# Full-width operations in the projection stage of an attention and FFN kernel, and a column sum taken from float32 tiles

## The chip, the cores and the metric

The kernel runs on all 8 NeuronCores of one Trainium2 chip. Each core takes 2 of the 16 sequences and does the whole computation on them; the cores exchange nothing. The metric is the device time in microseconds (us) of the slowest core.

## The reference

The input x is 16 sequences of 2048 tokens with 1024 features, in float32. The first half is an attention over the 16 heads of each single token, not over the tokens, and a layer norm:

```python
Q = (x @ Wq.T).reshape(b, s, h, hd)      # h = 16, hd = 64; K and V likewise
scores = jnp.einsum('bshd,bstd->bsht', Q, K) / math.sqrt(hd)
attn = jax.nn.softmax(scores, axis=-1)
out = jnp.einsum('bsht,bstd->bshd', attn, V).reshape(b, s, dm)
x = _layernorm(x + out @ Wfc.T)
```

The second half takes the mean of that x over the tokens of a sequence and puts it through a small net, which gives one number `gf` per sequence. Then three cycles follow, in which a four-layer net gives one number per token, and every token is updated with it:

```python
global_context = x.mean(axis=1, keepdims=True)
gf = _global_net(global_context, ...)
for _ in range(3):
    tf = _coupling_net(out, ...)
    coupling = 0.1 + adaptive_range * (0.7 * gf + 0.3 * tf - 0.5) * 2.0
    out = out + coupling * _twist(out)
x = _layernorm(x + out)
```

## The kernel before

Every engine has its own list of small functions, and the order in which Python appends to these lists is the order of the engine's queue. Waits are written out by hand, as semaphores with counts. Work is done one sequence (a batch of 2048 tokens) after the other, in three stages.

The **attention stage** takes the tokens in four blocks of 512. TensorE makes Q, K and V (L458); VectorE multiplies Q by shifted copies of K (L518, L524), and TensorE sums the products over the 64 features of a head with an indicator matrix (L544), which leaves the scores in `pS`, two PSUM banks of 512 columns. Then comes a chain in which each step waits for the one before: ScalarE takes the exponential of both banks into `praw` (`acE`, L565 and L566), TensorE sums it (L578, L579), ScalarE makes the reciprocals (L586 to L592), TensorE spreads them over the partitions with two float32 matmuls (L600, L601), VectorE multiplies (`dvN`, L610 and L611). After that TensorE spreads the weights (L643, 32 rows of the array), ScalarE copies them out (L659), VectorE multiplies them with V (L674), and TensorE sums again (L690, 64 columns of the array). The chain runs 8 times in all, 4 times for each batch.

The **projection stage** takes the tokens in 16 tiles of 128 (variable `tt`). For one tile TensorE does two groups of 8 full matmuls (`pe3`, L799), one for each half of the 1024 output columns, into two of the four banks of `pBIG`. VectorE adds the residual `x0f32` to each half (`dv2`, L811) into `sumtile`, takes mean and variance (`dv3`, L823 to L826), and ScalarE makes the reciprocal deviation (`ac3`, L834, L838). VectorE then writes the normalized tile twice (`dv4`): in float32 into `x1` (L849), which stays in SBUF for the rest of the batch, and in bfloat16 into `x1bfgc` (L852), a buffer for one tile. Two matmuls (`pe4`, L758 and L760) with a column of ones as stationary operand add the columns of `x1bfgc` into the sum over the tokens, of which the mean is made later. One tile's two matmuls accumulate on those of the tile before, in `pR` and `pA`.

The functions `dv4` and `pe4` of a tile are appended one tile late: VectorE's queue has `dv2` and `dv3` of tile tt, then `dv4` of tile tt-1; TensorE's queue has `pe3` of tile tt, then `pe4` of tile tt-1, then `pe3` of tile tt+1. For the last tile `dv4` also waits for the `pe4` before it (the count `gcg`). The sync engine's queue loads `x0f32` for tile tt when the additions of tile tt-1 are done.

The **FFN stage** transposes the tiles by DMA, runs the small net on the sum, and then runs the three cycles. It has its own epilogue with a layer norm, and is not touched by the change.

Of the kernel before, what the change touches and what calls it, by code (L numbers as in the profile page):

```python
# [7 lines left out]
F32 = mybir.dt.float32  # L8
BF16 = mybir.dt.bfloat16
AF = mybir.ActivationFunctionType  # L10
ALU = mybir.AluOpType
# [5 lines left out]
EXP_SCALE = 0.125  # L17
# [21 lines left out]
def build_nc():  # L39
# [31 lines left out]
    def at(name, shape, dtype, align=64):  # L71
        o = (off[0] + align - 1) // align * align
        t = nc.alloc_sbuf_tensor_at(name, shape, dtype, offset=BASE + o)
        nbytes = 1
        for s_ in shape[1:]:
            nbytes *= s_
        nbytes *= mybir.dt.size(dtype)
        off[0] = o + nbytes
        return t
# [4 lines left out]
    onesb = at("onesb", [128, 128], BF16)  # L84
# [4 lines left out]
    lncol = at("lncol", [128, 4], F32)  # L89
# [11 lines left out]
    expb = at("expb", [128, 1], F32)  # L101
# [9 lines left out]
    gw3sb = at("gw3sb", [128, 2], BF16)  # L111
    lnb = at("lnb", [8, 512], F32)
    idf32 = at("idf32", [128, 128], F32)
    tanhrow = at("tanhrow", [1, 256], F32)
    c4row = at("c4row", [1, 256], F32)
    assert off[0] <= 18000, off[0]
# [81 lines left out]
    pS = pBIG  # L198
# [70 lines left out]
    def ve_init(v):  # L269
        v.wait_ge(s_const.h, 1)  # L270
        v.memset(onesb[:, :], 1.0)
        v.memset(onesf[:, :], 1.0)
        v.memset(expb[:, :], EXP_BIAS)
        v.memset(epscol[:, :], LN_EPS)
        v.tensor_scalar(rcol[:, 1:2], rcol[:, 0:1], 64.0, None, ALU.is_ge)
        v.drain()
        for t in range(16):
            v.tensor_scalar(iwork2[:, 0:1], rcol[:, 1:2], 16.0, float(t), ALU.mult, ALU.add)
            v.drain()
            v.tensor_scalar(iwork2[:, 32:64], iwork[:, 0:32], iwork2[:, 0:1], None, ALU.is_equal)  # L280
            v.drain()
            v.tensor_copy(indt[:, t * 32: t * 32 + 32], iwork2[:, 32:64])
            v.drain()
        v.tensor_scalar(iwork2[:, 0:1], rcol[:, 1:2], -64.0, rcol[:, 0:1], ALU.mult, ALU.add)
        v.drain()
        v.tensor_scalar(iwork2[:, 1:65], iwork[:, 0:64], iwork2[:, 0:1], None, ALU.is_equal)
        v.drain()
        v.tensor_copy(redd[:, :], iwork2[:, 1:65])
        v.drain()
        v.tensor_scalar(iwork2[:, 0:1], rcol[:, 0:1], 1.0 / 16.0, None, ALU.mult)  # L290
        v.drain()
        v.tensor_scalar(iwork2[:, 8:16], iwork[:, 0:8], -1.0, iwork2[:, 0:1], ALU.mult, ALU.add)
        v.drain()
        v.tensor_scalar(iwork2[:, 16:24], iwork2[:, 8:16], 0.0, None, ALU.is_ge)
        v.tensor_scalar(iwork2[:, 24:32], iwork2[:, 8:16], 1.0, None, ALU.is_lt)
        v.drain()
        v.tensor_tensor(iwork2[:, 32:40], iwork2[:, 16:24], iwork2[:, 24:32], ALU.mult)
        v.drain()
        v.tensor_copy(rind[:, :], iwork2[:, 32:40])
        v.drain()  # L300
        v.tensor_scalar(iwork2[:, 0:128], iwork[:, 0:128], 1.0 / 16.0, None, ALU.mult)
        v.drain()
        v.tensor_scalar(iwork2[0:8, 0:128], iwork2[0:8, 0:128], rcol[0:8, 0:1], None, ALU.subtract)
        v.drain()
        v.tensor_scalar(iwork[0:8, 0:128], iwork2[0:8, 0:128], 0.0, None, ALU.is_ge)
        v.tensor_scalar(iwork2[0:8, 0:128], iwork2[0:8, 0:128], 1.0, None, ALU.is_lt)
        v.drain()
        v.tensor_tensor(e8[:, :], iwork[0:8, 0:128], iwork2[0:8, 0:128], ALU.mult)
        v.drain()
        nc.vector.engine_nop().then_inc(s_const.h, 1)  # L310
# [57 lines left out]
    for b in range(B_LOC):  # L368
# [26 lines left out]
        for sb_ in range(NSB):  # L395
# [165 lines left out]
            def acE(a, sacc_final=sacc_final, png=pnorm_gate_prev):  # L561
                a.wait_ge(s_sacc.h, sacc_final)
                if png > 0:
                    a.wait_ge(s_pnorm.h, png)
                a.activation(praw[:, 0:512], pS[:, 0:512], AF.Exp, bias=expb[:, :], scale=EXP_SCALE)  # L565
                a.activation(praw[:, 512:1024], pS[:, 512:1024], AF.Exp,  # L566
                             bias=expb[:, :], scale=EXP_SCALE).then_inc(s_exp2.h, 1)
            P.act.append(acE)
            exp_t = s_exp2.inc()
# [36 lines left out]
            def dvN(v, rexp_t=rexp_t, pfm_reuse=pfm_reuse):  # L606
                v.wait_ge(s_rexp.h, rexp_t)
                if pfm_reuse > 0:
                    v.wait_ge(s_pexp.h, pfm_reuse)
                v.tensor_tensor(pfm[:, 0:512], pBIG[:, 1024:1536], praw[:, 0:512], ALU.mult)  # L610
                v.tensor_tensor(pfm[:, 512:1024], pBIG[:, 1536:2048], praw[:, 512:1024],  # L611
                                ALU.mult).then_inc(s_pnorm.h, 1)
            P.dve.append(dvN)
            pnorm_t = s_pnorm.inc()
# [128 lines left out]
        def emit_dv4(gcg=0, P=P):  # L743
            fn, tt_p = pend_dv4[0]
            if gcg > 0:
                def wrapped(v, fn=fn, gcg=gcg):
                    v.wait_ge(s_gcs.h, gcg)
                    fn(v)
                P.dve.append(wrapped)
            else:  # L750
                P.dve.append(fn)
            x1_t = s_x1.inc()

            def pe4(te, x1_t=x1_t, tt=tt_p, rcp_gate=s_rcp2.n):
                te.wait_ge(s_x1.h, x1_t)
                if tt == 0:
                    te.wait_ge(s_rcp2.h, rcp_gate)
                m1 = te.matmul(pR[0:1, 0:512], onesb[:, 0:1], x1bfgc[:, 0:512],  # L758
                               start=(tt == 0), stop=(tt == NTT - 1))
                m2 = te.matmul(pA[0:1, 0:512], onesb[:, 0:1], x1bfgc[:, 512:1024],  # L760
                               start=(tt == 0), stop=(tt == NTT - 1))
                m2.then_inc(s_gcs.h, 1)
            P.pe.append(pe4)
            s_gcs.inc()
            pend_dv4[0] = None
            return x1_t

        for tt in range(NTT):
# [17 lines left out]
            for half in range(2):  # L786
                slot = slot0 + half
                bfree = fc_bank_free[slot]

                def pe3(te, tt=tt, half=half, slot=slot, ao_done=ao_done, bfree=bfree,  # L790
                        first=(tt == 0 and half == 0), wfc_tgt=wfc_tgt):
                    if first:
                        te.wait_ge(s_aoev.h, ao_done)
                        te.wait_ge(s_wf2.h, wfc_tgt)
                        te.wait_ge(s_winit.h, N_WINIT)
                    if bfree > 0:
                        te.wait_ge(s_sum.h, bfree)
                    for c in range(8):
                        mm = te.matmul(SLOT[slot],  # L799
                                       attnoutT[:, c * 2048 + tt * 128: c * 2048 + tt * 128 + 128],  # L800
                                       wfcsb[:, c * 1024 + half * 512: c * 1024 + half * 512 + 512],
                                       start=(c == 0), stop=(c == 7))
                    mm.then_inc(s_fc.h, 1)
                P.pe.append(pe3)
                fc_t = s_fc.inc()

                def dv2(v, fc_t=fc_t, x0f_t=x0f_t, half=half, tt=tt, slot=slot,
                        fsem=fsem, stile=stile):
                    v.wait_ge(s_fc.h, fc_t)
                    v.wait_ge(fsem.h, x0f_t)  # L810
                    v.tensor_tensor(stile[:, half * 512: half * 512 + 512],  # L811
                                    SLOT[slot],
                                    x0f32[:, (tt % 2) * 1024 + half * 512: (tt % 2) * 1024 + half * 512 + 512],
                                    ALU.add).then_inc(s_sum.h, 1)
                P.dve.append(dv2)
                sum_t = s_sum.inc()
                fc_bank_free[slot] = sum_t
            x0f_gate_prev = sum_t

            def dv3(v, sum_t=sum_t, par=par, stile=stile):  # L820
# [25 lines left out]
            def dv4(v, rstd_t=rstd_t, tt=tt, par=par, stile=stile):  # L846
                v.wait_ge(s_rstd.h, rstd_t)
                ag = aggr if par == 0 else aggr2
                v.tensor_scalar(x1[:, tt * 1024: tt * 1024 + 1024], stile[:, :],  # L849
                                ag[:, 0:1], lncol[:, par * 2 + 1: par * 2 + 2],  # L850
                                ALU.subtract, ALU.mult)
                v.tensor_scalar(x1bfgc[:, :], stile[:, :],  # L852
                                ag[:, 0:1], lncol[:, par * 2 + 1: par * 2 + 2],
                                ALU.subtract, ALU.mult)
                v.drain()
                nc.vector.engine_nop().then_inc(s_x1.h, 1)
# [658 lines left out]
```

## Time and profile before

| | |
|---|---|
| time, median of 3 runs | 3631.97 us (3628.18 to 3632.47) |
| the profiled execution's own time | 3658.85 us |
| its span on the slowest core | 3657.3 us (the fastest core: 3617.5 us) |
| granted TensorE clock, mean of the cores | 0.68 to 0.70 of full speed |
| PE, DVE, ACT busy | 66%, 37%, 32% of the span |
| projection stage, first batch | about 1008 to 1169 us |
| projection stage, second batch | about 2810 to 2978 us |

The profile is of one execution and one core (core 2). The clock column of the profile gives TensorE's granted clock as a share of 2.4 GHz: 1.00 is 2.4 GHz and 0.50 is 1.2 GHz. In the timeline a row is an instruction, or several of one kind merged, with its start and its length; what stands in brackets is how long the engine sat idle before it, and what ended that. Ends of matmuls are modelled, so for a chain of matmuls the distance between two starts says more than the lengths do.

### The profile page before, as it was taken

Reading aid. Unit: us, or ns where it says so; the run is one execution under the profiler, and the core shown is the slowest. Engines: PE = TensorE matmul, PEld = TensorE weight load, DVE = VectorE, ACT = ScalarE, POOL = GpSimd, SP = SyncE. Lnnn points to the kernel's source line nnn. Section 1 sums busy time; section 2 is a strip of 40 time slices with the busy share of each in tenths; the row PEclk is TensorE's granted clock in tenths of the full one; section 3 lists DMA queues with packets and bytes.
Section 4 is the critical chain, followed back from the end, with each engine's and each line's share of the span. In section 5 each row is a group of like instructions: output and inputs, shape, how many; then the busy total and the mean of one; then the engine's idle time right before and its main releaser. Section 6 shows DMA issues by size and latency. Waiting matters only on the chain.

```text
span 3657.3 us, 35637 instructions; the slowest of 8 cores (3617.5 to 3657.3 us)
## 1 busy us (share of the span) xinstructions
PE 2431.9 (66%) x10693; PEld 1064.8 (29%) x10736; DVE 1365.3 (37%) x2096; ACT 1163.9 (32%) x1848; POOL 37.6 (1%) x65
## 2 busy tenths in 40 slices
PE   0478788796754567575707887878876527585756
PEld 0221213122111345454503121221311105454544
DVE  2063544426343233333314425354343422423234
ACT  0125162442500233333301543516243003333333
POOL 1000000000000000000000000000000000000000
PEclk9955757575587777687757575565655867686877
DMA  6310100000112000100061001000001120101000
GB/s 90 57 33 1 21 1 1 1 1 12 21 49 53 9 18 18 35 5 31 3 109 35 18 3 19 1 1 1 12 1 29 52 46 4 35 3 33 8 28 24
DMA packets 110788, 83.88 MB, mean 23 GB/s; under 512 B 84496, under 2 KB 89104, under 8 KB 110608
## 3 DMA queue, kind: packets, MB, share of 16 engines
q0 software_dynamic: 19472, 31.21, 5.7%
q1 hardware_dynamic: 91136, 50.40, 4.8%
q8 instruction: 97, 1.59, 0.2%
q14 instruction: 83, 0.68, 0.1%
HBM read 79.18 MB, written 16.78 MB: 26 GB/s over the span
## 4 chain that ended last, share of the span: by engine, by line
PE 28%; DVE 5%; SPq 4%; DVEq 4%; issue 3%; ACT 3%; DMA 3%; ACTq 0%; POOLq 0%
PE pBIG L1151 5%; PE pQK L458 5%; PE pBIG L643 4%; SPq L934 3%; DVEq L514 2%; PE pBIG L799 2%; PE pQK L643 2%; PE pA L690 2%; PE pR L690 2%; PE pQK L1187 2%; SPq L424 1%; ACT pexpsb L659 1%; DMA outTbf<-xstg 1%; DMA x0tok<-x 1%; PE pBIG L544 1%
## 5 line engine op out<-in xcount | busy, mean ns | idle before, releaser
L674 DVE TENSOR_TENSOR prdsb<-pexpsb,vtsb 128x1024 bf16<-128x1024 bf16 x512 | 354.6, 693 | 534.3 <-ACT pexpsb L659 222.9
L1151 PE MATMUL pBIG<-outTbf,cw1sb 128*128 128x256 bf16 x3072 | 467.9, 327 | 41.4 <-ACT h1T L1164 41.3
L659 ACT ACTIVATE pexpsb<-pBIG 128x1024 bf16<-128x1024 f32 x344 | 349.2, 1023 | 159.3 <-PE pBIG L643 156.9
L1151 PEld LDWEIGHTS pBIG<-outTbf,cw1sb 128*128 128x128 bf16 x3072 | 344.7, 117 | 176.1 <-issue 69.6
L643 PE MATMUL pBIG<-pfm,expf 32*128 32x512 bf16 x688 | 345.4, 614 | 74.2 <-ACT pexpsb L659 60.8
L544 PE MATMUL pBIG<-prodb,indt 128*32 128x512 bf16 x1024 | 231.7, 550 | 144.9 <-DVE prodb L518 121.7
L458 PE MATMUL pQK<-x0T,wqsb 128*128 128x512 bf16 x497 | 129.5, 426 | 236.6 <-DMA x0T<-x0tok 233.8
L1164 ACT ACTIVATE h1T<-pBIG,cb1sb 128x256 bf16<-128x256 f32 x384 | 181.2, 473 | 261.9 <-PE pBIG L1151 261.8
L1187 PE MATMUL pQK<-h1T,cw2sb 128*128 128x256 bf16 x1536 | 182.4, 278 | 42.2 <-ACT h1T L1164 42.0
L510 DVE COPY kr<-ktsb 64x512 bf16<-64x512 bf16 x128 | 36.4, 285 | 440.5 <-ACT ktsb L471 438.6
L518 DVE TENSOR_TENSOR prodb<-qtsb,kr 128x2048 bf16<-128x2048 bf16 x128 | 156.8, 1225 | 101.5 <-PE pBIG L544 84.8
L643 PE MATMUL pQK<-pfm,expf 32*128 32x512 bf16 x336 | 172.6, 615 | 28.9 <-ACT pexpsb L659 28.9
L659 ACT ACTIVATE pexpsb<-pQK 128x1024 bf16<-128x1024 f32 x168 | 171.8, 1023 | 56.9 <-PE pQK L643 54.8
L1266 DVE TENSOR_SCALAR c4row<-tanhrow,abrow 1x256 f32<-1x256 f32 x48 | 19.2, 400 | 434.9 <-ACT tanhrow L1259 432.8
L544 PEld LDWEIGHTS pBIG<-prodb,indt 128*32 128x32 bf16 x1024 | 96.9, 100 | 279.2 <-issue 259.5
L690 PE MATMUL pR<-prdsb,redd 128*64 128x512 bf16 x512 | 162.7, 633 | 21.5 <-DVE prdsb L674 21.5
L799 PE MATMUL pBIG<-wfcsb,attnoutT 128*128 128x512 bf16 x500 | 152.0, 469 | 34.8 <-DMA wfcsb<-wfcT 33.4
L1187 PEld LDWEIGHTS pQK<-h1T,cw2sb 128*128 128x128 bf16 x1536 | 144.4, 99 | 80.2 <-issue 55.2
L690 PE MATMUL pA<-prdsb,redd 128*64 128x512 bf16 x512 | 162.8, 632 | 4.6 <-DVE prdsb L674 4.4
L1301 DVE TENSOR_TENSOR Ptw<-outT,C4N 128x512 f32<-128x512 f32 x192 | 119.8, 685 | 118.5 <-ACT C4N L1289 118.5
L524 DVE TENSOR_TENSOR prodb<-qtsb,kr 128x2048 bf16<-128x2048 bf16 x128 | 155.8, 1218 | 0.0
L458 PEld LDWEIGHTS pQK<-x0T,wqsb 128*128 128x128 bf16 x512 | 54.3, 108 | 311.1 <-issue 271.8
(176 smaller groups left out, 2024.7 us busy)
## 6 DMA issues: line engine op xcount, KB each, us to landing
x0f<-x SPq DMA_DIRECT2D x32, 512.0 KB, 3.2
out<-x2slab SPq DMA_DIRECT2D x32, 512.0 KB, 2.6
x0tok<-x POOLq DMA_DIRECT2D x32, 256.0 KB, 3.6
x0T<-x0tok SPq DMA_TRANSPOSE x256, 2.3
wqsb<-wqT POOLq DMA_DIRECT2D x2, 2048.0 KB, 18.6
wksb<-wkT POOLq DMA_DIRECT2D x2, 2048.0 KB, 30.5
wvsb<-wvT POOLq DMA_DIRECT2D x2, 2048.0 KB, 41.9
wfcsb<-wfcT POOLq DMA_DIRECT2D x2, 2048.0 KB, 16.3
```

Source lines behind the costliest of these rows:

```text
L458: mm = te.matmul(bank, wsb[:, (k * 8 + dch) * 128: (k * 8 + dch) * 128 + 128], x0T[:, par * 4096 + k * 512: par * 4096 + k * 512 + 512], s ...
L518: v.tensor_tensor(bass.AP(prodb, 0, [[4096, 128], [512, 4], [1, 512]]), bass.AP(qtsb, 0, [[4096, 128], [512, 4], [1, 512]]), krep, ALU.mul ...
L524: v.tensor_tensor(bass.AP(prodb, 2048, [[4096, 128], [512, 4], [1, 512]]), bass.AP(qtsb, 2048, [[4096, 128], [512, 4], [1, 512]]), krep, A ...
L544: mm = te.matmul(pS[32 * (c % 4): 32 * (c % 4) + 32, (c // 4) * 512: (c // 4) * 512 + 512], indt[:, t * 32: t * 32 + 32], prodb[:, c * 512 ...
L643: mm = te.matmul(pvb[:, hh * 512: hh * 512 + 512], expf[rb: rb + 32, (hh * 8 + k) * 128: (hh * 8 + k) * 128 + 128], pfm[rb: rb + 32, grp * ...
L659: a.activation(pexpsb[:, slot * 1024: slot * 1024 + 1024], pvb, AF.Copy).then_inc(s_pev.h, 1)
L674: v.tensor_tensor(bass.AP(prdsb, slot * 1024, [[2048, 128], [512, 2], [1, 512]]), bass.AP(pexpsb, slot * 1024, [[2048, 128], [512, 2], [1, ...
L690: te.matmul(rbank[hh * 64: hh * 64 + 64, :], redd[:, :], prdsb[:, slot * 1024 + hh * 512: slot * 1024 + hh * 512 + 512], start=(k == 0), s ...
L799: mm = te.matmul(SLOT[slot], attnoutT[:, c * 2048 + tt * 128: c * 2048 + tt * 128 + 128], wfcsb[:, c * 1024 + half * 512: c * 1024 + half ...
L1151: mm = te.matmul(SLOT[bank][:, 0:256], cw1sb[:, (k * 8 + dch) * 128: (k * 8 + dch) * 128 + 128], outTbf[:, k * 512 + hf * 256: k * 512 + h ...
L1164: a.activation(h1T[:, dch * 512 + hf * 256: dch * 512 + hf * 256 + 256], SLOT[bank][:, 0:256], AF.Gelu, bias=cb1sb[:, dch:dch + 1]).then_i ...
L1187: mm = te.matmul(pQK[:, q * 512: q * 512 + 256], cw2sb[:, (k * 4 + dch) * 128: (k * 4 + dch) * 128 + 128], h1T[:, k * 512 + hf * 256: k * ...
```

## The change

Four things are edited, and nothing else moves.

1. The exponential of the scores is one ScalarE instruction over 1024 columns, not two over 512.
2. The multiplication by the reciprocals (`dvN`) is one VectorE instruction over 1024 columns, not two.
3. The residual addition (`dv2`) of the projection stage is one instruction over 1024 columns. It is emitted after the second half's matmuls and waits for them, so the count on `s_sum` goes up once for each tile and not twice; both banks come free with it.
4. The bfloat16 copy `x1bfgc` is no longer written. `pe4` reads the float32 tile in `x1`, with a new float32 column of ones (`onec`, set once at the start) as stationary operand.

```diff
+    onec = at("onec", [128, 1], F32)
...
+        v.memset(onec[:, :], 1.0)
...
-                a.activation(praw[:, 0:512], pS[:, 0:512], AF.Exp, bias=expb[:, :], scale=EXP_SCALE)
-                a.activation(praw[:, 512:1024], pS[:, 512:1024], AF.Exp,
+                a.activation(praw[:, 0:1024], pS[:, 0:1024], AF.Exp,
                              bias=expb[:, :], scale=EXP_SCALE).then_inc(s_exp2.h, 1)
...
-                v.tensor_tensor(pfm[:, 0:512], pBIG[:, 1024:1536], praw[:, 0:512], ALU.mult)
-                v.tensor_tensor(pfm[:, 512:1024], pBIG[:, 1536:2048], praw[:, 512:1024],
+                v.tensor_tensor(pfm[:, 0:1024], pBIG[:, 1024:2048], praw[:, 0:1024],
                                 ALU.mult).then_inc(s_pnorm.h, 1)
...
-                m1 = te.matmul(pR[0:1, 0:512], onesb[:, 0:1], x1bfgc[:, 0:512],
+                m1 = te.matmul(pR[0:1, 0:512], onec[:, 0:1],
+                               x1[:, tt * 1024: tt * 1024 + 512],
                                start=(tt == 0), stop=(tt == NTT - 1))
-                m2 = te.matmul(pA[0:1, 0:512], onesb[:, 0:1], x1bfgc[:, 512:1024],
+                m2 = te.matmul(pA[0:1, 0:512], onec[:, 0:1],
+                               x1[:, tt * 1024 + 512: tt * 1024 + 1024],
                                start=(tt == 0), stop=(tt == NTT - 1))
...
+                if half == 1:
+                    def dv2(v, fc_t=fc_t, x0f_t=x0f_t, tt=tt, slot0=slot0,
+                            fsem=fsem, stile=stile):
+                        v.wait_ge(s_fc.h, fc_t)
+                        v.wait_ge(fsem.h, x0f_t)
+                        v.tensor_tensor(stile[:, :],
+                                        pBIG[:, slot0 * 512: slot0 * 512 + 1024],
+                                        x0f32[:, (tt % 2) * 1024: (tt % 2) * 1024 + 1024],
+                                        ALU.add).then_inc(s_sum.h, 1)
+                    P.dve.append(dv2)
+                    sum_t = s_sum.inc()
+                    fc_bank_free[slot0] = sum_t
+                    fc_bank_free[slot0 + 1] = sum_t
...
-                v.tensor_scalar(x1bfgc[:, :], stile[:, :],
-                                ag[:, 0:1], lncol[:, par * 2 + 1: par * 2 + 2],
-                                ALU.subtract, ALU.mult)
```

On VectorE, one tile in the middle of the projection stage (x1 stands as `x_113`, x0f32 as `x0f`) was this:

```order
L811 TENSOR_TENSOR sumtile<-pBIG,x0f_96 128x512 x2
L823 BN_STATS stats<-sumtile 128x6
L824 BN_STATS stats<-sumtile 128x6
L826 BN_AGGR aggr<-stats 128x2
L828 ISA
L849 TENSOR_SCALAR x_113<-sumtile_87,aggr_47,lncol 128x1024
L852 TENSOR_SCALAR x1bfgc<-sumtile_87,aggr_47,lncol 128x1024
L856 ISA
```

and is now this, with x1 as `x_114`:

```order
L814 TENSOR_TENSOR sumtile<-pBIG,x0f_97 128x1024
L827 BN_STATS stats<-sumtile 128x6
L828 BN_STATS stats<-sumtile 128x6
L830 BN_AGGR aggr<-stats 128x2
L832 ISA
L853 TENSOR_SCALAR x_114<-sumtile_88,aggr_47,lncol 128x1024
L857 ISA
```

The two additions have become one of twice the width, and one of the two full-width writes is gone. The order is otherwise the same.

On TensorE the same stage, from its first matmuls, was this:

```order
L799 MATMUL pBIG<-wfcsb,attnoutT 128x512 x32
L758 MATMUL pR<-x1bfgc,onesb 1x512
L760 MATMUL pA<-x1bfgc,onesb 1x512
L799 MATMUL pBIG<-wfcsb,attnoutT 128x512 x16
L758 MATMUL pR<-x1bfgc,onesb 1x512
L760 MATMUL pA<-x1bfgc,onesb 1x512
```

and is now this:

```order
L801 MATMUL pBIG<-wfcsb,attnoutT 128x512 x32
L758 MATMUL pR<-x_114,onec 1x512
L761 MATMUL pA<-x_114,onec 1x512
L801 MATMUL pBIG<-wfcsb,attnoutT 128x512 x16
L758 MATMUL pR<-x_114,onec 1x512
L761 MATMUL pA<-x_114,onec 1x512
```

No matmul has moved; the two of `pe4` read float32 operands of the same shapes.

## Rows read from the trace of the kernel before

**Rows 1.** The page: engines, and the clock over 40 slices.
```profile
PE 2431.9 (66%) x10693; PEld 1064.8 (29%) x10736; DVE 1365.3 (37%) x2096; ACT 1163.9 (32%) x1848; POOL 37.6 (1%) x65
PEclk9955757575587777687757575565655867686877
```
**Rows 2.** Timeline, one settled tile of the projection stage.
```profile
1042.12 0.58 PE L758 MATMUL pR<-x1bfgc,onesb 128*1 128x512 bf16 x1 [4.55 <-DVEq L856]
1042.49 0.63 PE L760 MATMUL pA<-x1bfgc,onesb 128*1 128x512 bf16 x1
1043.06 4.70 PE L799 MATMUL pBIG<-wfcsb,attnoutT 128*128 128x512 bf16 x16
...
1046.21 0.69 DVE L811 TENSOR_TENSOR sumtile<-pBIG,x0f 128x512 f32<-128x512 f32 x1 [4.34 <-PE pBIG L799]
1047.93 0.69 DVE L811 TENSOR_TENSOR sumtile<-pBIG,x0f 128x512 f32<-128x512 f32 x1 [1.03 <-PE pBIG L799]
...
1050.53 0.81 DVE L849 TENSOR_SCALAR x<-sumtile,aggr,lncol 128x1024 f32<-128x1024 f32 x1 [0.18 <-issue]
...
1051.26 0.81 DVE L852 TENSOR_SCALAR x1bfgc<-sumtile,aggr,lncol 128x1024 bf16<-128x1024 f32 x1
...
1052.31 0.59 PE L758 MATMUL pR<-x1bfgc,onesb 128*1 128x512 bf16 x1 [4.55 <-DVEq L856]
```
**Rows 3.** Stretches: start and end, length, then busy time of each engine, clock, DMA.
```profile
1035.10:1041.80 6.70, 2.47 (x12) 0.91 (x10) 4.34 (x7) 0.50 (x2) 0.00 (x0) 1.00 0.23 78
1041.90:1045.20 3.30, 3.08 (x8) 0.88 (x9) 0.00 (x0) 0.00 (x0) 0.00 (x0) 0.50 0.00 0
1045.30:1052.00 6.70, 2.46 (x12) 0.89 (x10) 4.35 (x7) 0.50 (x2) 0.00 (x0) 1.00 0.25 78
2827.10:2833.80 6.70, 5.67 (x14) 1.81 (x15) 1.37 (x2) 0.00 (x0) 0.00 (x0) 0.50 0.00 0
240.00:250.00 10.00, 9.59 (x26) 1.54 (x24) 4.84 (x7) 8.01 (x9) 0.53 (x1) 0.50 0.24 43
```
**Rows 4.** Timeline, first and last column sums of each batch.
```profile
1021.28 0.52 PE L758 MATMUL pR<-x1bfgc,onesb 128*1 128x512 bf16 x1 [4.66 <-DVEq L856]
1154.67 0.59 PE L758 MATMUL pR<-x1bfgc,onesb 128*1 128x512 bf16 x1 [4.55 <-DVEq L856]
1164.90 0.59 PE L758 MATMUL pR<-x1bfgc,onesb 128*1 128x512 bf16 x1 [4.55 <-DVEq L856]
1166.10 0.81 DVE L849 TENSOR_SCALAR x<-sumtile,aggr,lncol 128x1024 f32<-128x1024 f32 x1 [1.43 <-PE pA L760]
2828.13 0.59 PE L758 MATMUL pR<-x1bfgc,onesb 128*1 128x512 bf16 x1 [4.66 <-DVEq L856]
2829.07 5.97 PE L799 MATMUL pBIG<-wfcsb,attnoutT 128*128 128x512 bf16 x16
2974.05 0.58 PE L758 MATMUL pR<-x1bfgc,onesb 128*1 128x512 bf16 x1 [4.54 <-DVEq L856]
```
**Rows 5.** Groups by line: a float32 addition over 1024 columns.
```profile
L1388 DVE TENSOR_TENSOR sumtile<-x,sumtile 128x1024 f32<-128x1024 f32 x32 | 39.2, 1225 | 5.6 <-ACT sumtile L1378 3.1 <-issue 2.4
```
**Rows 6.** Timeline, the chain from the scores to the weights, first block.
```profile
228.23 0.69 ACT L565 ACTIVATE praw<-pBIG,expb 128x512 bf16<-128x512 f32 x1 [46.60 <-PE pBIG L544]
228.81 0.68 ACT L566 ACTIVATE praw<-pBIG,expb 128x512 bf16<-128x512 f32 x1
...
233.54 2.04 PE L600 MATMUL pBIG<-rcpf,e 8*128 8x512 f32 x2 [2.88 <-ACT rcpf L592]
...
235.37 1.91 PE L601 MATMUL pBIG<-rcpf,e 8*128 8x512 f32 x2
...
237.39 0.69 DVE L610 TENSOR_TENSOR pfm<-pBIG,praw 128x512 bf16<-128x512 f32 x1 [10.66 <-PE pBIG L601]
238.00 0.68 DVE L611 TENSOR_TENSOR pfm<-pBIG,praw 128x512 bf16<-128x512 f32 x1
```
**Rows 7.** Groups by line: ScalarE copies from PSUM of 1024 and of 512 columns.
```profile
L659 ACT ACTIVATE pexpsb<-pBIG 128x1024 bf16<-128x1024 f32 x344 | 349.2, 1023 | 159.3 <-PE pBIG L643 156.9 <-DVE prdsb L674 0.6
L471 ACT ACTIVATE ktsb<-pQK 128x512 bf16<-128x512 f32 x64 | 38.2, 597 | 77.6 <-PE pQK L458 77.6
```
**Rows 8.** Timeline, TensorE after the last column sum of batch 1.
```profile
1212.17 0.35 PE L984 MATMUL pQK<-onesb,gcrow 1*128 1x1 bf16 x8 [43.28 <-DVEq L978]
```
**Rows 9.** Timeline, the load of the residual for the next tile.
```profile
1038.51 10.52 SPq L779 DMA_DIRECT2D x0f<-x  x2
```

More of the change, by code:

```diff
@@ L805, in build_nc @@
                 fc_t = s_fc.inc()
[L807 to L817, printed above, removed]
+                if half == 1:
[11 more added lines that the diff above has]
+                    fc_bank_free[slot0 + 1] = sum_t
             x0f_gate_prev = sum_t
```

## The prediction

> **What bounds the kernel now.** I read the page first. TensorE is the busiest engine with 66% of the span, VectorE and ScalarE have 37% and 32%, and the clock row swings between 5 and 9 tenths [rows 1]. No engine is full, so a stage is set by chains of waits, and by which level of the clock TensorE has there. Each edit has to be read in its own stage.
>
> Next I read the timeline of one settled tile of the projection stage [rows 2]. It is a ring of serial work. TensorE starts `pe4` at 1042.12 and the 16 full matmuls (L799) at 1043.06, whose last ends just before VectorE's second addition at 1047.93. VectorE then adds, takes statistics and writes the previous tile twice, and only the end of the second write (L852) releases the next `pe4`, at 1052.31. In front of it TensorE has sat idle for 4.55 us. The ring takes 10.19 us: 0.94 for `pe4`, about 4.7 for the full matmuls, 4.55 for VectorE with TensorE idle. So every 0.1 us that VectorE loses behind the last full matmul, or TensorE gains in `pe4`, is paid 0.1 us a tile, unless the clock moves too.
>
> The clock does move. Between 1035.10 and 1041.80 it was 1.00 (2.4 GHz), between 1041.90 and 1045.20 it was 0.50 (1.2 GHz), then 1.00 again to 1052.00 [rows 3]. It falls near the end of TensorE's idle time, `pe4` and the first five or so full matmuls run at 1.2 GHz, and it comes back 2.2 us after the first full matmul. In the first tile of batch 2 the low stretch lasted from 2827.10 to 2833.80, because `pe4` began 1.1 us after the fall [rows 3, 4]: the clock came back only 4.8 us after the first full matmul (2829.07), and the 16 of them took 5.97 us instead of 4.70 [rows 4]. So the later in a low stretch the full matmuls start, the longer it lasts, and that is worth more than a microsecond.
>
> What raises the clock is not TensorE being busy as such. From 240 to 250 us it is busy for 9.59 us of 10 and the clock stays at 0.50 [rows 3]; the work there uses 32 rows (L643) or 64 columns (L690) of the array. `pe4` uses one column. I take it that `pe4` does nothing for the clock, in bfloat16 or in float32.
>
> **The change part by part.** *The additions.* Before, half of the addition was done while the second half's matmuls ran; 0.69 us stood behind them [rows 2]. Now all of it does. The same kind of operation over 1024 columns takes 1.225 us [rows 5]. So +0.53 us a tile in the ring. Behind the waiting addition on VectorE stand the statistics and `dv4`, all in the ring already. The bank of the first half comes free later, but it is needed only two tiles on. SP's load of the next residual is issued at the end of the addition, so 0.53 us later; it was issued at 1038.51 for additions from 1046 on [rows 2, 9], and stays hidden.
>
> *The second write.* L849 starts at 1050.53 and L852 at 1051.26 [rows 2]; without L852 the release comes that much earlier: −0.73 us a tile. TensorE's idle time becomes 4.55 + 0.53 − 0.73 = 4.35 us.
>
> *The column sums.* The trace shows no float32 matmul with one column. The nearest rows are L600 and L601, float32 over 512 columns at a clock of 1.2 GHz: each runs as two records, and the first starts 1.83 us before the second [rows 6]. A float32 matmul there costs over four times what a bfloat16 one does (0.38 from L758 to L760 [rows 2]). Their weights are 128 columns wide and here they are one, so I take 1.75 us each, 3.5 us for the pair, against 0.94 now: +2.55 us a tile at 1.2 GHz. The bounds are 0.94 us (float32 costs nothing here) and 3.7 us; at 2.4 GHz the pair would be near 1.8 us.
>
> *The full matmuls behind them.* Here the larger half of the uncertainty lies. With the fall where it is now or earlier, 3.5 us of one-column work at 1.2 GHz stand ahead of the full matmuls, so these begin later in the low stretch than in any tile of the trace, and the tile nearest to it is the first of batch 2, with 4.8 us of low clock behind the first full matmul and 5.97 us for the sixteen. The ends are 3.4 us (sixteen at 2.4 GHz: 16 × 0.215, from the spacing of the second half, 1.72 us between the two additions of a tile) and 6.8 us (all at 1.2 GHz). I take 5.8, a little under the row. That is +1.1 us a tile.
>
> The ring becomes 4.35 + 3.5 + 5.8 = 13.65 us. Its ends: 4.35 + 1.8 + 3.4 = 9.6 and 4.35 + 3.7 + 6.8 = 14.9.
>
> *Over the stage.* From the first `pe4` to the fifteenth are 14 rings in each batch: 1164.90 − 1021.28 = 143.6 us and 2974.05 − 2828.13 = 145.9 us now [rows 4]. With the first ring or two of each batch shorter before it settles, I take 189.5 us for each: +45.9 and +43.6, together +89.5 us. At the end `dv4` of the last tile waits for the fifteenth `pe4`: it started 1.20 us behind it [rows 4], now some 3.7, less the second write: +2.5 − 0.7 = +1.8 for each batch, +3.6. The last `pe4` itself is off the path: TensorE then waits 43.28 us for transposes by DMA and VectorE [rows 8]. The first tile's addition costs +0.4 for each batch, +0.8, before the ring begins.
>
> *The attention stage.* The exponentials take from 228.23 to 229.49, 1.26 us [rows 6]. A copy of 1024 columns takes 1.023 us, and the exponential needs 0.09 more than a copy (0.69 against 0.597) [rows 6, 7]: 1.11 us, −0.15. The multiplications take from 237.39 to 238.68, 1.29 us, against 1.225 [rows 5]: −0.07. Both stand on a chain that nothing covers, since the engines around them wait. Eight times −0.22 is −1.8 us. They can't lose more than they were.
>
> Sum: 89.5 + 3.6 + 0.8 − 1.8 = +92 us. On the profiled execution's 3658.85 us that is 3751; it was 27 us slower than the median, and 3631.97 + 92 = **3724 us**.
>
> **The rivals.** *A: float32 column sums raise the clock.* If 3.5 us of unbroken one-column work counted as activity, the clock would come back before the full matmuls: 4.35 + 3.5 + 3.4 = 11.3 us a ring, +1.1 × 28 = +31, and with the small terms +33: 3665 us. Rows 240 to 250 speak against it: nearly full, and at 0.50. The Trainium skill speaks for it: "TensorE: Matmul & The Clock Gate", Part 1, says that the activity monitor gates the clock on how busy the engine has been, and that sustained matmuls release it. By that rule alone the ring would be 11.3 us; the trace doesn't bear it out where the array is partly used. A mixed case, in which the rise alternates between early and late, lies around 12 us a ring, +50: 3684.
>
> *B: the clock never falls.* TensorE's idle time shrinks to 4.35 us. The last full matmul of the tile ended before 1047.93, and the clock was still 1.00 until 1052.00, over 4.1 us later [rows 2, 3], so the margin is small. If 4.35 us of idle time were too short for a fall, all would run at 2.4 GHz and the ring be 9.6 us, −0.6 × 28 = −17; the ends of the stages give nothing, the attention stage −1.8: −19 us, 3613, faster than before. It decides from the point where no fall shows in the idle time. Against it: what the clock has to be kept up by is the full matmuls, and between these now lie 4.35 + 1.8 = 6.2 us instead of 5.5.
>
> *C: float32 with one column costs as bfloat16.* Then the ring is 0.2 us shorter at most, −6 − 2: 3624; or, since the fall seems to hold the ring where it is (it crept up to 10.23 us, from 1154.67 to 1164.90 [rows 4]), −2: 3630. L600 and L601 speak against it.
>
> **How the numbers follow.** The forecast has a chance of 0.78, A with the mixed case 0.14, B 0.04, C 0.04. The forecast's own range is +78 (the clock returns a little earlier) to +108 us (settled from the first ring, on every core): 3710 to 3740. To leave out no more than 2 in 10 I go down to the mixed case, 3680, and up to 3748. What a measurement can tell from no change is 0.2%, 7 us. Faster by more: B and half of C, 0.05. Within: the rest of C, 0.03. Slower: 0.92.
>
> **What would show it.** Right: L758 and the second column sum appear as four records a tile, 3.4 to 3.6 us from the first to the first full matmul at a clock of 0.50; a ring of 13 to 13.7 us; TensorE's idle before L758 at 4.35; sixteen full matmuls at 5.5 to 6; two additions gone for one of 1.23 us; 46 us more between first and fifteenth `pe4` of a batch; all else unchanged. Wrong: `pe4` near 1 us (C), a clock of 1.00 at the first full matmul (A), or a clock of 1.00 all through a tile (B). The forecast would also fail if the stage's clock settled into another pattern, for which the trace of before gives no row.

## The result, and the profile after

The changed kernel takes 3699.69 us (median of 9 runs, 3681.84 to 3727.03), the kernel before 3632.22 us in the same sessions. The ratio is 1.0166, with a 95% interval from 1.0141 to 1.0191: about 60 us slower. In some executions one die of the chip has a lower clock and the time is 1 to 3% longer; the ratios leave these out, the medians don't. The forecast was slower by 92 us, 3724 us, in a range from 3680 to 3748. The direction and the place were right, and one step of the sum, the full matmuls behind the column sums, was too large.

The profile after is of core 7, with a span of 3692.3 us. These rows of its page answer to [rows 1]:

```profile
PE 2478.6 (67%) x10800; PEld 1054.6 (29%) x10800; DVE 1336.6 (36%) x2025; ACT 1163.8 (32%) x1840; POOL 37.5 (1%) x65
```

TensorE is busy 47 us longer and VectorE 29 us shorter; the two pages are of different cores, so this is rough. Next the timeline after: two tiles of the projection stage, matmuls and VectorE's addition. They answer to [rows 2].

```profile
1059.44 1.87 PE L758 MATMUL pR<-x,onec 128*1 128x512 f32 x2 [4.36 <-DVEq L857]
1061.10 1.91 PE L761 MATMUL pA<-x,onec 128*1 128x512 f32 x2
1062.94 4.45 PE L801 MATMUL pBIG<-wfcsb,attnoutT 128*128 128x512 bf16 x16
...
1067.58 1.22 DVE L814 TENSOR_TENSOR sumtile<-pBIG,x0f 128x1024 f32<-128x1024 f32 x1 [8.38 <-PE pBIG L801]
...
1070.70 0.81 DVE L853 TENSOR_SCALAR x<-sumtile,aggr,lncol 128x1024 f32<-128x1024 f32 x1 [0.18 <-issue]
...
1071.75 1.86 PE L758 MATMUL pR<-x,onec 128*1 128x512 f32 x2 [4.36 <-DVEq L857]
1073.41 1.76 PE L761 MATMUL pA<-x,onec 128*1 128x512 f32 x2
1075.11 3.63 PE L801 MATMUL pBIG<-wfcsb,attnoutT 128*128 128x512 bf16 x16
```

The float32 column sums appear as four records a tile and last from 1059.44 to 1062.94, 3.50 us, and from 1071.75 to 1075.11, 3.36 us. TensorE's idle time in front is 4.36 us. Both were forecast to within 0.15 us. The 16 full matmuls, though, take 4.45 and 3.63 us, in turn, and not 5.8. The stretches of the clock in the same two tiles answer to [rows 3] (length, busy time of PE, PEld, DVE, ACT, POOL, clock, DMA):

```profile
1057.90:1064.60 6.70, 5.16 (x8) 0.95 (x9) 1.05 (x3) 0.50 (x2) 0.00 (x0) 0.50 0.18 65
1064.70:1071.40 6.70, 2.70 (x13) 1.02 (x11) 3.42 (x5) 0.50 (x2) 0.00 (x0) 1.00 0.24 72
1071.50:1074.80 3.30, 3.05 (x4) 0.36 (x4) 0.01 (x1) 0.00 (x0) 0.00 (x0) 0.50 0.02 6
1074.90:1081.70 6.80, 3.84 (x17) 1.49 (x16) 2.56 (x4) 0.00 (x0) 0.00 (x0) 1.00 0.09 17
```

In the first tile the clock is at 1.2 GHz until 1.7 us behind the first full matmul (1062.94). In the second it is back at 2.4 GHz before the first full matmul at 1075.11, and in the low stretch in front of that rise (1071.50 to 1074.80) TensorE had done nothing but column sums.

From the first tile's column sum to the fifteenth's, which is 14 rings, it is now 165.6 us in the first batch and 167.6 us in the second:

```profile
1036.90 1.46 PE L758 MATMUL pR<-x,onec 128*1 128x512 f32 x2 [4.47 <-DVEq L857]
1202.47 1.01 PE L758 MATMUL pR<-x,onec 128*1 128x512 f32 x1 [4.36 <-DVEq L857]
```
```profile
2849.55 0.77 PE L758 MATMUL pR<-x,onec 128*1 128x512 f32 x1 [4.47 <-DVEq L857]
3017.18 1.86 PE L758 MATMUL pR<-x,onec 128*1 128x512 f32 x2 [4.36 <-DVEq L857]
```

In [rows 4] it was 143.6 and 145.9. A single core can mislead by a microsecond or two, so from here on "14 rings" is the median over 8 cores and both batches, from the starts of the same matmuls. The time and the spans hold the other stages too, which vary from core to core by more than some of the effects looked for; the rings don't. The last four rows are versions with another order in TensorE's queue, explained at the end of the next section.

| kernel | idle before the sums, us | 14 rings, us | one ring | time against before, ratio (95%) |
|---|---|---|---|---|
| before | 4.55 | 144.4 | 10.32 | |
| changed | 4.36 | 166.4 | 11.89 | 1.0166 (1.0141 to 1.0191) |
| edits 1 and 2 alone | 4.55 | 144.7 | 10.34 | 0.9994 (0.9962 to 1.0026) |
| edit 3 alone | 5.08 | 158.4 | 11.31 | 1.0097 (1.0069 to 1.0125) |
| edit 4 alone | 3.82 | 155.8 | 11.13 | 1.0225 (1.0150 to 1.0300) |
| second write left out | 3.82 | 132.6 | 9.47 | 0.9924 (0.9879 to 0.9969) |
| bfloat16 four times, 128 rows | 4.36 | 166.2 | 11.87 | no ratio |
| bfloat16 four times, 32 rows | 4.36 | 190.8 | 13.63 | 1.0254 (1.0119 to 1.0388) |
| sums one tile later, bfloat16 | 0.9 | 71.6 | 5.12 | 0.9549 (0.9466 to 0.9632) |
| sums one tile later, float32 | 0 | 74.2 | 5.30 | 0.9570 (0.9494 to 0.9646) |
| the same, edits 1 to 3, copy on ScalarE | up to 1.4 | 68.2 | 4.87 | 0.9558 (0.9432 to 0.9684) |
| the same, sums two tiles later | 0 | 57.6 | 4.12 | 0.9520 (0.9461 to 0.9580) |

So the rings cost 2 × 22.0 = 44 us more. At the end of each batch the last tile's column sum starts 4.8 us behind the fifteenth's instead of 2.97 us, +1.8 each. That makes 48 of the 60 us. Where the other 12 come from is in part a matter of the slowest core. From the first full matmul of the stage to its last column sum the median core needs 186.4 and 187.0 us in the two batches, against 161.4 and 162.3 before, +50 in all, and the fastest executions of the two kernels differ by 55 us (3681.84 and 3626.95). In the profiled execution core 7, the slowest, begins its first full matmul at 1023.7 us and the median core at 1007.2. What makes that core late, and the few microseconds outside the stage, are left open.

### The profile page after: what moved, and what is told of

Same layout as the page of the kernel before. It is cut to its first block and busy times, and to the rows that moved or that the text cites. A ratio compares the mean times of both kernels' runs of the same rounds, so it can differ in the third digit from the quotient of the medians.

```text
span 3692.3 us, 35665 instructions; the slowest of 8 cores (3668.6 to 3692.3 us)
## 1 busy us (share of the span) xinstructions
PE 2478.6 (67%) x10800; PEld 1054.6 (29%) x10800; DVE 1336.6 (36%) x2025; ACT 1163.8 (32%) x1840; POOL 37.5 (1%) x65
## 5 line engine op out<-in xcount | busy, mean ns | idle before, releaser
L1152 PE MATMUL pBIG<-outTbf,cw1sb 128*128 128x256 bf16 x3072 | 459.4, 322 | 43.6 <-ACT h1T L1165 43.5
L659 ACT ACTIVATE pexpsb<-pBIG 128x1024 bf16<-128x1024 f32 x344 | 349.6, 1024 | 158.6 <-PE pBIG L643 156.5
L643 PE MATMUL pBIG<-pfm,expf 32*128 32x512 bf16 x688 | 345.4, 614 | 73.7 <-ACT pexpsb L659 60.8
L643 PE MATMUL pQK<-pfm,expf 32*128 32x512 bf16 x336 | 172.6, 615 | 28.6 <-ACT pexpsb L659 28.6
L659 ACT ACTIVATE pexpsb<-pQK 128x1024 bf16<-128x1024 f32 x168 | 172.1, 1024 | 56.7 <-PE pQK L643 54.7
L690 PE MATMUL pR<-prdsb,redd 128*64 128x512 bf16 x512 | 162.7, 633 | 21.3 <-DVE prdsb L674 21.3
L690 PE MATMUL pA<-prdsb,redd 128*64 128x512 bf16 x512 | 162.7, 631 | 4.9 <-DVE prdsb L674 4.7
L801 PE MATMUL pBIG<-wfcsb,attnoutT 128*128 128x512 bf16 x512 | 132.3, 418 | 33.7 <-DMA wfcsb<-wfcT 33.7
L758 PE MATMUL pR<-x,onec 128*1 128x512 f32 x64 | 58.1, 1010 | 133.4 <-DVEq L857 133.4
```

Source lines behind the costliest of these rows:

```text
L643: mm = te.matmul(pvb[:, hh * 512: hh * 512 + 512], expf[rb: rb + 32, (hh * 8 + k) * 128: (hh * 8 + k) * 128 + 128], pfm[rb: rb + 32, grp * ...
L659: a.activation(pexpsb[:, slot * 1024: slot * 1024 + 1024], pvb, AF.Copy).then_inc(s_pev.h, 1)
L690: te.matmul(rbank[hh * 64: hh * 64 + 64, :], redd[:, :], prdsb[:, slot * 1024 + hh * 512: slot * 1024 + hh * 512 + 512], start=(k == 0), s ...
L801: mm = te.matmul(SLOT[slot], attnoutT[:, c * 2048 + tt * 128: c * 2048 + tt * 128 + 128], wfcsb[:, c * 1024 + half * 512: c * 1024 + half ...
L1152: mm = te.matmul(SLOT[bank][:, 0:256], cw1sb[:, (k * 8 + dch) * 128: (k * 8 + dch) * 128 + 128], outTbf[:, k * 512 + hf * 256: k * 512 + h ...
```

## The experiments

**Edits 1 and 2 alone.** Only the wide exponential and the wide multiplication.

```diff
+                a.activation(praw[:, 0:1024], pS[:, 0:1024], AF.Exp,
...
+                v.tensor_tensor(pfm[:, 0:1024], pBIG[:, 1024:2048], praw[:, 0:1024],
```

> Only edits 1 and 2 (the exponential and the multiplication over 1024 columns in one instruction). Theory: both stand on an uncovered chain, so 8 x (0.15 + 0.07) = 1.8 us less, which is 0.05% and cannot be told from no change by the time; the exponential should read 1.11 us and the multiplication 1.23 in the trace, and the projection stage keep its rings of 10.2 us. Rival: the wider instructions change when the clock falls in the attention stage, then whole blocks of that stage (213 us each) move by several us.

Measured: ratio 0.9994 (0.9962 to 1.0026), no change that can be told. The rings stay (144.7 us for 14). The rival doesn't show: the first full matmul of the projection stage starts at 1007.0 us in the median core, and at 1008.3 in the kernel before. The two groups of its profile have the lengths that were forecast:

```profile
L609 DVE TENSOR_TENSOR pfm<-pBIG,praw 128x1024 bf16<-128x1024 f32 x8 | 9.8, 1225 | 84.3 <-PE pBIG L600 84.3
L565 ACT ACTIVATE praw<-pBIG,expb 128x1024 bf16<-128x1024 f32 x8 | 8.9, 1113 | 371.9 <-PE pBIG L544 371.9
```

That is 1.11 and 1.225 us, against 1.26 and 1.29 for the pairs [rows 6]. A gain of 1.7 us in all (8 × 0.21) follows from these and is too small for the time to confirm.

**Edit 3 alone.** The residual addition in one instruction (the third part of the change's diff).

> Only edit 3 (the residual addition in one instruction). TensorE's idle time grows from 4.55 to 5.08 us. Theory that the clock's falls pace the ring: TensorE starts later after each fall, drifts out of step every few tiles, rings of 10.3 to 12.0 us that repeat, mean 10.3 to 10.8, 1 to 8 us more over 14 rings, +3 to +16 us in all. Rival, plain addition: every ring 0.53 us longer, 10.75 each, and +15 us in all.

Measured: 14 rings take 158.4 us, +14.0 for each batch, +28 in all; the time says 1.0097. Both expectations were too low. Two of its tiles:

```profile
1080.14 0.59 PE L758 MATMUL pR<-x1bfgc,onesb 128*1 128x512 bf16 x1 [5.08 <-DVEq L858]
...
1081.08 6.12 PE L799 MATMUL pBIG<-wfcsb,attnoutT 128*128 128x512 bf16 x16
...
1092.28 0.59 PE L758 MATMUL pR<-x1bfgc,onesb 128*1 128x512 bf16 x1 [5.08 <-DVEq L858]
...
1093.22 5.18 PE L799 MATMUL pBIG<-wfcsb,attnoutT 128*128 128x512 bf16 x15
```
```profile
1079.40:1086.10 6.70, 5.96 (x14) 1.90 (x15) 0.50 (x1) 0.00 (x0) 0.00 (x0) 0.50 0.00 0
1089.70:1096.30 6.60, 4.02 (x10) 1.26 (x11) 2.08 (x4) 0.50 (x2) 0.00 (x0) 0.50 0.22 79
1103.30:1106.60 3.30, 3.12 (x8) 0.92 (x9) 0.00 (x0) 0.00 (x0) 0.00 (x0) 0.50 0.00 0
```

The idle time is 5.08 us, as worked out: +0.53. But the full matmuls now take 6.12, 5.18 and 4.7 us in turn, where they took 4.70 before. The clock is still at 0.50 for 5.0, 3.1 and 2.2 us behind the first full matmul (1081.08, 1093.22 and 1104.42 in the third tile), against 2.2 us in the kernel before (1043.06 to about 1045.2 [rows 2, 3]). So the addition is charged twice: once as idle time, and once because the clock stays low further into the full matmuls.

**Edit 4 alone.** Column sums in float32, one write, two additions (the second and fourth part of the change's diff).

> Only edit 4 (column sums in float32 from x1, no bfloat16 copy), additions as before in two. TensorE's idle time should be 3.82 us. Theory that float32 sums count for the clock, and that a shorter idle time lets it stay up more often: rings of 10.2 to 10.8 us with a longer one now and then, +1.5 to +7 us over 14 rings, and with the ends of the stages +7 to +18 us in all. Rival, plain subtraction from the changed kernel: its rings of 11.42 and 12.47 us less 0.53, mean 11.4, so +17 us over 14 rings and +37 us in all.

Measured: 155.8 us, +11.4 for each batch; one ring 11.13. It lies between the two expectations, nearer to the plain one (11.4). Rings of 10.9, 10.87, 10.56 and 12.04 us repeat. The ratio of 1.0225 would be 82 us, and the rings and the ends of the two stages account for only 26 of them, so it says slower and no more.

**The second write left out.** The kernel before with one write; its column sums read a weight tile, so the sum over the tokens is left out.

```diff
-                v.tensor_scalar(x1bfgc[:, :], stile[:, :],
...
-                m1 = te.matmul(pR[0:1, 0:512], onesb[:, 0:1], x1bfgc[:, 0:512],
+                m1 = te.matmul(pR[0:1, 0:512], onesb[:, 0:1], wfcsb[:, 0:512],
```

> The kernel before without the bfloat16 write (VectorE, 0.73 us a tile in the ring); its two column sums read the weight tile wfcsb in the place of x1bfgc, so the sum over the tokens is left out and TensorE's work stays the same. TensorE's idle time should be 3.82 us instead of 4.55. Theory that the clock's falls pace the ring near 10.24 us: rings of 9.5 to 10.5 us at first, then back to 10.2, 1 to 2 us less over 14 rings, -2 to -6 us in all. Rival, plain subtraction, as the prediction had it: -0.73 x 28 = -20 us and another -1.5 at the ends of the stages.

Measured: 132.6 us, −11.8 for each batch, −0.84 a ring for 0.73 us less of VectorE; ratio 0.9924 (0.9879 to 0.9969). My theory here, that the clock holds the ring near 10.24 us whatever VectorE does, is wrong; the plain subtraction (−20 us) comes nearer to the −23.6 us of the rings. With 3.82 us of idle time some falls of the clock don't come at all:

```profile
1097.77 0.38 PE L758 MATMUL pR<-wfcsb,onesb 128*1 128x512 bf16 x1 [3.82 <-DVEq L853]
...
1098.29 3.63 PE L799 MATMUL pBIG<-wfcsb,attnoutT 128*128 128x512 bf16 x16
...
1105.74 0.38 PE L758 MATMUL pR<-wfcsb,onesb 128*1 128x512 bf16 x1 [3.82 <-DVEq L853]
```
```profile
1097.80:1105.70 7.90, 4.12 (x18) 1.54 (x18) 3.69 (x6) 0.50 (x2) 0.00 (x0) 1.00 0.20 67
```

This ring took 7.97 us, all at 2.4 GHz. The ring before it took 10.39.

**Bfloat16 in the place of float32.** The changed kernel with four bfloat16 matmuls of one column for each float32 one. They read a weight tile, so the sum over the tokens is left out.

```diff
+                for r in range(4):
+                    m1 = te.matmul(pR[0:1, 0:512], onesb[:, 0:1], wfcsb[:, 0:512],
+                                   start=(tt == 0 and r == 0), stop=(tt == NTT - 1 and r == 3))
```

> The changed kernel, but each float32 column sum is replaced by four bfloat16 matmuls of 512 columns with the same column of ones, which read the weight tile wfcsb: the sum over the tokens is left out, the work of TensorE in pe4 stays as long (8 x 0.427 = 3.4 us at 1.2 GHz, against 3.5). Theory 1, it is the float32 passes that raise the clock and bfloat16 with one column does nothing for it: full matmuls start at 1.2 GHz and take 5.7 us, rings settle at 13.65 us, about +90 us over the kernel before. Theory 2, any unbroken work of that length raises it: full matmuls of 3.6 and 4.5 us in turn, rings of 11.4 and 12.5, about +50 us, as in the changed kernel.

Measured: 166.2 us, the changed kernel's 166.4. The type of the data makes no difference, and theory 1 is out. The word "any" in theory 2 goes further than this run, as the next one shows. Two tiles:

```profile
1081.24 1.86 PE L759 MATMUL pR<-wfcsb,onesb 128*1 128x512 bf16 x4 [4.36 <-DVEq L857]
...
1084.65 3.63 PE L801 MATMUL pBIG<-wfcsb,attnoutT 128*128 128x512 bf16 x16
...
1092.63 1.87 PE L759 MATMUL pR<-wfcsb,onesb 128*1 128x512 bf16 x4 [4.36 <-DVEq L857]
...
1096.14 4.60 PE L801 MATMUL pBIG<-wfcsb,attnoutT 128*128 128x512 bf16 x16
```

**The same over 32 rows.** As the last one, but ones and weights are taken from 32 partitions.

```diff
+                for r in range(4):
+                    m1 = te.matmul(pR[0:1, 0:512], onesb[0:32, 0:1], wfcsb[0:32, 0:512],
+                                   start=(tt == 0 and r == 0), stop=(tt == NTT - 1 and r == 3),
+                                   tile_position=(0, 0))
```

> The kernel with four bfloat16 matmuls in the place of each float32 column sum, but these use only 32 of the array's 128 rows (32 partitions of ones and of the weight tile); same count, same 512 columns, same length. The sum over the tokens is left out. Theory: what keeps the clock low in the stretch 240 to 250 us is that the matmuls use few rows, and the width of the output (one column) is no matter. Then these 3.5 us leave the clock low, full matmuls take 5.6 to 5.9 us, rings settle at 13.6 us and the time is about 90 us over the kernel before, as was forecast for the changed kernel. Rival: any matmul of that length counts alike: rings of 11.4 and 12.5 us in turn, about +50 us.

Measured: 190.8 us, one ring 13.63; ratio 1.0254 (1.0119 to 1.0388). The column sums take the same 3.5 us as over 128 rows, and the clock stays low behind them:

```profile
1086.28 1.86 PE L759 MATMUL pR<-wfcsb,onesb 32*1 32x512 bf16 x4 [4.36 <-DVEq L859]
...
1089.78 5.81 PE L803 MATMUL pBIG<-wfcsb,attnoutT 128*128 128x512 bf16 x16
...
1099.95 1.86 PE L759 MATMUL pR<-wfcsb,onesb 32*1 32x512 bf16 x4 [4.36 <-DVEq L859]
```
```profile
1086.30:1089.70 3.40, 3.40 (x8) 0.80 (x8) 0.00 (x0) 0.00 (x0) 0.00 (x0) 0.50 0.02 6
1089.80:1093.00 3.20, 3.20 (x9) 1.16 (x9) 0.00 (x0) 0.00 (x0) 0.00 (x0) 0.50 0.00 0
```

This kernel behaves as was forecast for the changed one: full matmuls of 5.81 us (5.8), rings of 13.67 (13.65), 190.8 us over 14 rings (189.5). The only difference to the experiment before is the number of rows (with the place in the array that goes with it). The ratio rests on two executions, but the rings of the profiled one agree on all 8 cores and in both batches (190.2 to 191.7 us).

**The sums one tile later, bfloat16.** The kernel before, with `pe4` put one tile later into TensorE's queue, and a second buffer. `dv4` waits for the sum that used its buffer.

```diff
-            P.pe.append(pe4)
...
+            pend_pe4.append(pe4)
...
+        def emit_pe4():
+            P.pe.append(pend_pe4.pop(0))
             s_gcs.inc()
...
+            if pend_pe4:
+                emit_pe4()
             if pend_dv4[0] is not None:
                 x1_final = emit_dv4()
```

> The kernel before, with the column sums one tile later in TensorE's queue (behind the full matmuls of the next tile but one) and two bfloat16 buffers in turn. Theory that the stage is a ring and no engine is full: TensorE no longer waits for VectorE in front of the column sums, the tile is set by VectorE (0.69 for the first addition + 4.14 from the second addition to the end of the second write + gaps = 5.0 us), about 5.2 us less than 10.2 for 28 tiles, -140 us. Rival: the load of the residual, which is issued only when the additions of the tile before are done, or a lower clock in unbroken work (0.81) takes the place: 6 to 7 us a tile, -90 to -115 us.

Measured: 3485.48 us, ratio 0.9549 (0.9466 to 0.9632). Most rings take 5.04 us, as worked out from VectorE's rows, and 14 of them 71.6: 146 us less in both batches, where 140 were expected. The rival, 6 to 7 us a tile, is out.

```profile
1052.90 0.38 PE L762 MATMUL pR<-x1bfgc,onesb 128*1 128x512 bf16 x1 [1.15 <-DVEq L867]
...
1052.91 1.29 DVE L818 TENSOR_TENSOR sumtile<-pBIG,x0f 128x512 f32<-128x512 f32 x2 [0.24 <-issue]
...
1053.43 3.63 PE L806 MATMUL pBIG<-wfcsb,attnoutT 128*128 128x512 bf16 x16
...
1057.94 0.38 PE L762 MATMUL pR<-x1bfgc,onesb 128*1 128x512 bf16 x1 [0.88 <-DVEq L867]
```

TensorE's idle time is 0.88 to 1.15 us instead of 4.55, VectorE no longer waits for TensorE, and the matmuls are at 2.4 GHz (3.63 us for the sixteen).

**The sums one tile later, float32.** The changed kernel with the same deferral.

> The changed kernel with the same deferral (no second buffer is needed, the sums read x1; the last tile's write no longer waits for the sum before). Theory: VectorE needs 4.2 us a tile, TensorE 1.8 + 3.5 = 5.3 us at 2.4 GHz and 6.5 at 0.81 of it; TensorE sets the tile, -100 to -135 us against the kernel before. Here the second write that edit 4 saves is worth nothing, and the float32 sums cost 1.3 us a tile more than bfloat16: slower than the deferral with bfloat16 sums if the clock is below 2.4 GHz, within 10 us of it if not.

Measured: 3496.11 us, ratio 0.9570 (0.9494 to 0.9646). Rings take 5.37 us with TensorE never idle, where 5.3 were expected at 2.4 GHz. That is 0.33 us more than with bfloat16 sums, and not 1.3, because with bfloat16 VectorE sets the tile and TensorE has the time to spare.

```profile
1054.72 1.02 PE L759 MATMUL pR<-x,onec 128*1 128x512 f32 x2
...
1055.57 1.02 PE L762 MATMUL pA<-x,onec 128*1 128x512 f32 x2
...
1056.53 3.63 PE L805 MATMUL pBIG<-wfcsb,attnoutT 128*128 128x512 bf16 x16
```

At 2.4 GHz the pair takes 1.81 us (1054.72 to 1056.53), the price that the prediction named for that level. Here edit 4 costs its plain length and nothing by the clock.

**Deferral, edits 1 to 3, the copy on ScalarE.**

```diff
+            def acC(a, x1_t=x1_t, tt=tt_p, gcs0=gcs0):
+                a.wait_ge(s_x1.h, x1_t)
...
+                a.activation((x1bfgc if tt % 2 == 0 else x1bfgc2)[:, :],
+                             x1[:, tt * 1024: tt * 1024 + 1024],
+                             AF.Copy).then_inc(s_xbf.h, 1)
...
-            gate = 0 if tt < 2 else x0f_gate_prev
+            gate = 0 if tt < 2 else sum_hist[tt - 2]
```

The load of the residual is also issued one tile earlier (the last two lines).

> The deferral with bfloat16 sums, edits 1 to 3, the bfloat16 copy made by ScalarE from x1 (1.0 us, ScalarE is idle there), and the residual's load issued one tile earlier. Theory: VectorE 1.22 + 1.3 + 0.2 + 0.8 and gaps = 4.1 us a tile, TensorE 0.43 + 3.43 = 3.9 us at 2.4 GHz or 4.8 at 0.81: 4.2 to 4.9 us a tile, -150 to -170 us against the kernel before. Rival: something not in this sum (the load of 512 KB for each tile, the latency of the deviation on ScalarE) holds it at the time of the plain deferral.

Measured: 3505.53 us, ratio 0.9558 (0.9432 to 0.9684), not to be told by the time from the plain deferral; the 14 rings are 3.5 us shorter (68.2 for 71.6). In the first batch rings alternate between 4.18 and 5.53 us, in the second half of the second batch between 4.53 and 5.18. In the short ones TensorE is nearly without a gap; in the long ones it waits in front of the sum for ScalarE's copy (L760), and VectorE then waits for TensorE:

```profile
1063.87 0.38 PE L771 MATMUL pR<-x1bfgc,onesb 128*1 128x512 bf16 x1 [1.38 <-ACT x1bfgc L760]
...
1068.20 1.23 DVE L828 TENSOR_TENSOR sumtile<-pBIG,x0f 128x1024 f32<-128x1024 f32 x1 [1.59 <-PE pBIG L815]
```

**The sums two tiles later.** The same with three buffers.

```diff
-            if pend_pe4:
+            if len(pend_pe4) > 1:
                 emit_pe4()
```

> The kernel with the deferral, edits 1 to 3 and the copy on ScalarE, whose column sums come one tile later still, with three buffers in turn. In the profile of the version with one tile less the rings alternate between 4.18 and 5.53 us, because TensorE waits up to 1.4 us for ScalarE's copy (L760) in front of the column sum. Theory: that wait goes, VectorE (4.1 us) and TensorE (3.9) alternate without gaps, rings of 4.2 to 4.3, another -0.6 x 28 = -17 us, about -180 us against the kernel before. Rival: the two halves' banks come free only after the one wide addition, and TensorE waits for those instead: rings stay at 4.8.

Measured: 3458.97 us (3457.03 to 3484.68), ratio 0.9520 (0.9461 to 0.9580). The wait is gone; rings take 4.08 to 4.18 us, but for one of 4.36 in the second batch. The rival, rings of 4.8, is out.

```profile
1064.29 0.38 PE L773 MATMUL pR<-x1bfgc,onesb 128*1 128x512 bf16 x1
...
1064.82 3.63 PE L817 MATMUL pBIG<-wfcsb,attnoutT 128*128 128x512 bf16 x15
...
1068.47 0.38 PE L773 MATMUL pR<-x1bfgc,onesb 128*1 128x512 bf16 x1
```

This version has the lowest median of all. By the ratios it is about 175 us faster than the kernel before and 235 us faster than the changed one; 2 × (144.4 − 57.6) = 174 us of it are the rings. Between 1064.29 and 1068.47 TensorE has no idle time at all.

## Why the prediction was right in sign and too large

- *The ring, and the idle time in it.* Right: 4.36 us for 4.35. The deferral shows the ring itself: without the long wait for VectorE the tile falls from 10.3 to 5.04 us, with the same work on every engine.
- *The float32 sums.* Right: 3.36 to 3.50 us for 3.5.
- *The small terms.* The end of a batch came out as summed up, 4.80 for 2.97 us, +1.8. The +0.4 us for the first tile's addition doesn't show: from the first full matmul to the first column sum it is 13.80 us in the median, and was 13.75.
- *The addition and the second write.* Their lengths were right. Their worth in the ring was not: I charged +0.53 and −0.73, and in the kernel before they are worth +1.0 (edit 3 alone) and −0.84 us a ring. The idle time counts more than once, because it also decides when the clock falls and how much of the work behind it runs at 1.2 GHz.
- *The full matmuls behind the sums.* This step failed. I took them at 5.8 us, and they take 3.63 and about 4.6 us in turn. That is 1.7 us a ring, 2 × 14 × 1.7 = 48 us, and the gap between the forecast's 89.5 us for the rings and the 44 measured is this term.
- *The reason that I gave for it.* "I take it that `pe4` does nothing for the clock" rested on the stretch 240 to 250 us, where TensorE is busy and the clock stays low [rows 3], and I carried that over to one column. One column over 128 rows raises the clock (experiment with bfloat16 four times), and one column over 32 rows doesn't, in work of the same length. In that stretch 14 of the 26 matmuls are L643's over 32 rows, and the other 12 L690's over 128 rows with 64 columns. That L643's rows are what holds the clock down there fits these two experiments, but no run changes one of the two groups alone.
- *The rivals.* The measured stage is the mixed case of rival A, in which the rise comes early in one tile and late in the next; I had put it near 12 us a ring (settled, it is 11.42 and 12.47 in turn) and gave A with it 0.14. So it was luck that the time fell into the range: the forecast's own range was 3710 to 3740, and the 3699.69 lies in the wider one only because its lower end was drawn down to the mixed case. What the forecast had taken to happen behind the sums, with its chance of 0.78, isn't what the trace shows. By the rule of "TensorE: Matmul & The Clock Gate" in the Trainium skill, Part 1, that the engine's being busy releases the clock, the one-column sums should count, and here the trace agrees (full matmuls of 3.63 and 4.60 us behind the bfloat16 ones). It doesn't agree for the 32 rows: TensorE is busy for 3.40 of 3.40 us there and the clock stays at 0.50 for another 3.2. Rivals B and C are ruled out by the clock rows and by the 3.5 us of the sums. By the prices given, B and half of C make 0.06 for faster, where I wrote 0.05.
- *The edits, taken apart.* From the kernel before, the write left out −0.84, float32 sums +1.66 (9.47 to 11.13), wide addition +0.76 (11.13 to 11.89): together 10.32 to 11.89 us a ring. I had +3.65 for the float32 sums with what they do to the full matmuls.
- *The attention stage.* A gain of 1.7 us follows from the lengths (1.8 forecast), and the time can't confirm it.

## What to carry to other kernels

Where TensorE waits in a ring with another engine, look at the order of its queue before the cost of any instruction: putting the two small matmuls one tile later took the kernel from 3632 to 3485 us. Two tiles later, with the wide addition, the copy on an idle engine and the earlier load, it was worth 175 us, and all the edits of the change together moved the rings by 44 the wrong way. In such a ring a microsecond of idle time is not worth a microsecond, since it also moves the clock: measure rings, and take the clock into the sum on both sides. Joining two half-width instructions into one saved 0.07 to 0.15 us where nothing ran beside the first half (edits 1 and 2), and cost 1.0 us a ring where the first half had run beside matmuls (edit 3).

## What the runs showed of the hardware

- Matmuls with a single output column over all 128 rows brought TensorE's clock back from 1.2 to 2.4 GHz. The same number of matmuls over 32 rows, just as long (3.5 us), didn't: full matmuls behind them took 5.81 us in the settled tiles, against 3.63 and 4.60.
- A float32 matmul with one output column and 512 moving columns took 1.66 us at 1.2 GHz (1059.44 to 1061.10) and 0.85 at 2.4 GHz (1054.72 to 1055.57). Eight bfloat16 ones took 3.41 us (1081.24 to 1084.65) where the float32 pair took 3.36 to 3.50, so one float32 matmul costs as much as four in bfloat16.
- Edit 3 added 0.53 us of idle time to a ring and lengthened it by 1.0 us; leaving out the second write took 0.73 us away and shortened it by 0.84, and some of its rings, of 7.97 us, had no stretch of low clock at all.
- Settled rings repeat to about 0.01 us on all cores, in patterns of one (13.65 us, 32 rows), two (11.42 and 12.47, changed), three (10.73, 12.18 and 11.22, edit 3 alone) or four tiles (edit 4 alone). Those of the kernel before creep to 10.24 us. Nothing in the work differs from tile to tile; what differs is where in the tile the clock changes.
